# First keys in a software pipeline on VectorE, and pads of the first values cleared on ScalarE

## Reference

```python
kv = (cond @ Wkv + bkv).reshape(1, -1, 2, H, hd)     # 16 heads of 16
k, v = kv[:, :, 0], kv[:, :, 1]
k = _fq_sym(k, axis=-1)      # per row and head: s = max|k|/127, round(k/s)*s
v = _fq_sym(v, axis=2)       # per channel: the maximum runs over all 12808 rows
attn = softmax(einsum('bhqd,bhkd->bhqk', q, k)); out = einsum(attn, v)
```

## Time and profile before

| what | value |
|---|---|
| median of 3 runs | 6314.11 us (6314.06 to 6315.52) |
| the profiled execution's own time | 6316.26 us |
| its span in the trace | 6314.5 us |
| granted clock of PE, mean | 0.938 |
| busy: PE, DVE, ACT, POOL | 5663.1, 5327.8, 4621.8, 3820.7 us |

### The profile page before, as it was taken

The page is one execution under the profiler, slowest core; times in us unless marked ns, Lnnn a source line. Parts: engine busy times, 40 slices in busy tenths (PEclk is TensorE's granted clock), DMA queues, the critical chain, the costliest instruction groups (busy, mean ns, idle before and its releaser), DMA issues. The chain is left out here.

```text
span 6314.5 us, 180489 instructions
## 1 busy us (share of the span) xinstructions
PE 5663.1 (90%) x64257; PEld 2223.0 (35%) x64264; DVE 5327.8 (84%) x8826; ACT 4621.8 (73%) x4630; POOL 3820.7 (61%) x4116
## 2 busy tenths in 40 slices
PE   8787399999999999999999999999999694699974
PEld 5565123333323332332332332333233443354442
DVE  4187799999989998999999998999899535577778
ACT  4466039999989998998998998999899321366644
POOL 5433138888888887888888888888888200100000
PEclk9899569999999999999999999999999797799987
DMA  6655400100101101001011010110110101877750
GB/s 230 258 133 123 133 15 10 26 15 17 26 8 25 20 11 27 15 17 24 7 28 19 12 26 11 22 22 8 28 17 13 38 1 34 125 116 114 114 93 21
DMA packets 178691, 315.60 MB, mean 50 GB/s; under 512 B 91555, under 2 KB 137636, under 8 KB 173170
## 3 DMA queue, kind: packets, MB, share of 16 engines
q1 hardware_dynamic: 177768, 303.45, 22.9%
HBM read 198.26 MB, written 113.07 MB: 49 GB/s over the span
## 5 line engine op out<-in xcount | busy, mean ns | idle before, releaser
L1426 DVE TENSOR_REDUCE a_mx<-PS 128x1 f32<-128x512 f32 x6620 | 3984.5, 679 | 220.2 <-PE PS L1310 216.5
L1397 ACT ACTIVATE a_e<-PS,a_sk 126x1024 f32<-126x1024 f32 x3264 | 3630.6, 1113 | 386.2 <-PE PS L1293 133.0
L1164 POOL TENSOR_SCALAR a_p<-a_e 126x1024 f16<-126x1024 f32 x3264 | 3410.4, 1045 | 570.3 <-ACT a_e L1397 345.3
L1310 PE MATMUL PS<-a_K,a_Q 48*128 48x512 bf16 (+1 forms) x6884 | 2106.8, 383 | 33.1 <-POOL a_K L1129 32.4
L1293 PE MATMUL PS<-a_Q,a_K 54*128 54x512 bf16 x6528 | 1979.0, 383 | 33.5 <-issue 24.2
L1337 PE MATMUL PS<-a_e,a_sel 126*32 126x256 f32 x26112 | 1990.6, 381 | 0.0
L1333 PE MATMUL PS<-a_p,a_V 128*32 128x256 f16 x13056 | 959.0, 284 | 44.6 <-issue 32.2
L1293 PEld LDWEIGHTS PS<-a_Q,a_K 54*128 54x128 bf16 x6528 | 369.3, 94 | 1384.1 <-issue 1321.5
L1333 PEld LDWEIGHTS PS<-a_p,a_V 128*32 128x32 f16 x13056 | 337.3, 93 | 1376.2 <-issue 1291.5
L1337 PEld LDWEIGHTS PS<-a_e,a_sel 126*32 126x32 f32 x26112 | 755.4, 110 | 7.9 <-issue 1.4
L2326 DVE TENSOR_REDUCE b_mx<-PS 128x1 f32<-128x512 f32 x803 | 504.3, 683 | 188.3 <-PE PS L2210 188.1
(11 more groups left out here) (339 smaller groups left out, 3454.7 us busy)
## 6 DMA issues: line engine op xcount, KB each, us to landing
b_K<-d_k SPq DMA_DIRECT2D x210, 200.1 KB, 6.1
a_K<-d_k SPq DMA_DIRECT2D x99, 400.2 KB
b_V<-d_v SPq DMA_DIRECT2D x36, 832.0 KB, 12.2
d_k<-k_T SPq DMA_DIRECT2D x100, 252.0 KB, 4.4
d_k<-k1p SPq DMA_DIRECT2D x16, 1200.8 KB, 6.1
d_v<-v1v SPq DMA_DIRECT2D x24, 768.0 KB, 7.8
a_V<-d_v SPq DMA_DIRECT2D x68, 204.0 KB, 2.9
d_v<-vq SPq DMA_DIRECT2D x17, 803.2 KB
```

The lines of the kernel that those rows point to most:

```text
L1164: g.tensor_scalar(p[0:rows, kk % RE, :], e[0:rows, kk % RE, :], 1.0, SHIFT, ALU.mult, ALU.add).then_inc(rounded, 1)
L1310: last = pe.matmul(self.PS[:, M_BANK + j % sh.SLOTS, c0:c0 + wd], Qb[M_ROWS, ii % 4, t * P:(t + 1) * P], Kb[M_ROWS, (ii // NC) % 2, k0:k0 ...
L1397: a.activation(e[0:r, kk % RE, :], self.PS[0:r, e_bank(i, s):e_bank(i, s) + 2, :], ACT.Exp, scale=skb[0:r, hb, s:s + 1]).then_inc(exp_done, 1)
L1426: v.tensor_reduce(mx[:, col:col + 1], bank, AX.X, ALU.max).then_inc(max_done, 1)
```

## The change

1. First keys, DVE: no operation waits for the one just before it. Each raises a semaphore of its own (`k_largest`, `k_scale`, `rk_ready`, ...), and the next one of the same group stands two or more operations later in the queue, with operations of the two or three groups before in between. The separate semaphore instructions are gone. The group's last part is made three rounds after its maximum.
2. The buffers of parts (`parts`, `ip`) are four instead of two (RP = 4), and PE turns group g-4 behind kv(g), instead of g-2.
3. First keys, ACT: values(g), evacuate(g-4), high(g-1), middle(g-2).
4. PE waits only for the four clearings of `pick`, and DVE splits the bias before it waits for POOL's clearings.
5. First values: POOL no longer clears `vq`. ACT writes zeros to the 16-column pads alone, and PE's sums and SP's first store wait for that. The rounding operations raise `done` themselves. ACT issues 17 of the 34 corrections' DMAs.
6. First attention: the pad of `Kb` is cleared before `p`, and PE waits for `init` at 4, without `p`.

```diff
-            RC = 6
+            RC, RP = 6, 4
...
-                pe.wait_ge(zeroed, 10)
+                pe.wait_ge(zeroed, 4)
...
-                    if g >= 2:
-                        turn(g - 2)
-                turn(NG - 2)
-                turn(NG - 1)
+                    if g >= 4:
+                        turn(g - 4)
+                for g in range(NG - 4, NG):
+                    turn(g)
...
+                def over(g, op, signal):
+                    todo = spans(g)
+                    for s, n in todo[:-1]:
+                        self.link(v, op(s, n), self.dv)
+                    op(*todo[-1]).then_inc(signal, 1)
...
+                for g in range(NG + 3):
+                    when(g, largest_key)
+                    when(g - 1, whole)
+                    when(g, scale)
+                    when(g - 1, larger_value)
+                    when(g, reciprocal)
+                    when(g - 1, scaled)
+                    when(g, multiplied)
+                    when(g - 2, rest)
+                    when(g - 3, last)
...
+                for g in range(NG + 4):
+                    when(g, values)
+                    when(g - 4, evacuate)
+                    when(g - 1, high)
+                    when(g - 2, middle)
...
-                g.memset(vq[:, :, :, :], 0.0).then_inc(zeroed, 1)
...
+                a.activation(vq[:, :, :, HD:2 * HD].rearrange("p h t d -> p (h t) d"), along(self.onesf[:, 0:HD], 1, HEADS // 2 * NKT),
+                             ACT.Copy, scale=0.0).then_inc(pads, 1)
+                a.wait_ge(ready, 1)
+                store_corrections(a, 1)
...
-                g.memset(p[96:P, :, :], SHIFT).then_inc(init, 1)
                 g.memset(Kb[0:E_ROWS, :, sh.NK:sh.NK + PAD], 0.0).then_inc(init, 1)
+                g.wait_ge(init, 4)
+                g.memset(p[96:P, :, :], SHIFT).then_inc(init, 1)
...
-                pe.wait_ge(init, 5)
+                pe.wait_ge(init, 4)
```

More of the change, by code:

```diff
@@ L800, in scales, with reciprocal @@
+                def reciprocal(g):
+                    v.wait_ge(k_scale, g + 1)
                     if g >= 2:
                         v.wait_ge(ip_ready, g - 1)
[L802 to L808, removed]
-                        if s.stop == GT:
-                            v.sem_inc(rk_ready, 1)
-                        self.link(v, v.tensor_tensor(by_head(tmp[0:n, b, s, :]), by_head(ps), along(rc, 3, HD), ALU.mult), self.dv)
@@ L843, in scaled @@
-                def scaled(g):
-                    b = g % 2
-                    for s, n in spans(g):
-                        sc = sk[0:n, :, g * GT + s.start:g * GT + s.stop].rearrange("p h t -> p t h")
-                        self.link(v, v.tensor_tensor(by_head(kf[0:n, b, s, :]), by_head(parts[0:n, b, INT, s, :]), along(sc, 3, HD), ALU.mult), self.dv)
-                    v.sem_inc(to_cast, 1)
-                for g in range(NG):
-                    scales(g)
-                    if g >= 1:
-                        rest(g - 1)
-                    whole(g)
-                    if g >= 1:
-                        last(g - 1)
-                    scaled(g)
-                    largest(g)
@@ L859, in _, with multiplied @@
-                rest(NG - 1)
-                last(NG - 1)
+                    over(g, lambda s, n: v.reciprocal(rk[0:n, g % 2, s, :], scale_of(g, s, n)), rk_ready)
+                def multiplied(g):
+                    v.wait_ge(rk_ready, g + 1)
+                    if g >= 2:
+                        v.wait_ge(k_whole, g - 1)
+                    over(g, lambda s, n: v.tensor_tensor(by_head(tmp[0:n, g % 2, s, :]), by_head(keys_of(g, s, n)),
+                                                         along(rk[0:n, g % 2, s, :], 3, HD), ALU.mult), kv_seen)
@@ L862, in _ @@
+                v.wait_ge(v_larger, NG)
             @block.scalar
@@ L896, in _, with when @@
                 a.wait_ge(zeroed, 10)
[L897 to L909 removed]
+                def when(g, op):
+                    if 0 <= g < NG:
+                        op(g)
+                for g in range(NG + 4):
[3 more added lines that the diff above has]
+                    when(g - 2, middle)
     def first_values(self):
@@ L1026, in _ @@
                 sp.wait_ge(ready, 1)
[L1027 to L1031 removed]
+                store_corrections(sp, 0)
                 sp.wait_ge(stored, 16 * (17 + 2 * (HEADS + 1)))
```

130 lines of the change are left out of this document (67 added, 63 removed).

## The result

| kernel | median (lowest to highest), runs | against before, 95% interval |
|---|---|---|
| before | 6314.82 us (6314.06 to 6318.07), 4 | |
| changed | 6220.11 us (6216.75 to 6225.9), 4 | 0.985 (0.9833 to 0.9867) |

What follows compares the result with a forecast made beforehand. It took DVE's chain to hold a first-keys group at 6.27 us, with PE the next bound. Keys -61.2, start +1.4, values -26.6 and attention -5.2 sum to -91.6 us: 6222.5 from 6314.1, range 6208 to 6248 (0.8).

Steps and rivals of the forecast that it cites:

- Keys, -61.2: First keys: the stage from PE's first product to ACT's last copy falls from 334.2 to 273.0 us.
- P = 4.97: First keys: time of one steady group, 4.97 us instead of 6.27, counted for 46 groups.
- POOL's lock: First keys: POOL and DVE exclude each other for whole operations, costing DVE from nothing to five times 0.1 us.
- The groups without turns and the tail: First keys: first group 7.1 us, four groups without turns 15.6, and a tail of four turns with copies 21.7.
- Start, +1.4: Start of the first keys: DVE's cast is held by POOL's clearing of `k_parts`, so PE begins 1.4 us later.
- Values, -26.6: First values: no clearing of `vq` and corrections issued by two queues; the end comes at 703.7 instead of 730.3 us.
- one shared pace: First values: alternative in which both issuers of the corrections share one pace, so the gain is -19.8 us.
- Attention, -5.2: Start of the first attention: PE is released by loads of `a_K` at about 739 instead of 744.26 us.
- (a): First keys: DVE becomes the bound at 5.5 us a group, stage 298 us, kernel 6247.5; chance 0.17 with its halfway case.
- (b): First keys: POOL starves between DVE's operations, a group takes 8.8 us and the kernel 6413; chance 0.03.
- (c): First keys: stores or loads bound, a group takes 5.6 us and the kernel is near 6252; chance 0.07.
- (d): Whole kernel: the changed stages do not hold what they promise and the time stays near 6314 us; chance 0.02.

Runs made afterwards that it cites:

- linked version: The changed kernel with every DVE operation of the first keys also waiting for its own end before the next may start; 6249.23 us.
- version with additions: The changed kernel with ACT clearing `k_parts`, second-half roundings waiting only for their own head's store, and turns of groups 48 and 50 in free banks; 6216.14 us.
- single parts: Three kernels, each the kernel before with only the changed first keys, first values or order of POOL's clearings in the first attention; 6251.1, 6291.49 and 6303.91 us.

## Why the prediction was right

**What bounds.** Right: DVE's chain before, PE after. I had traced PE's wait of 1.16 us back over ACT to a late DVE, and then still spoke of it as something that ACT's order takes away. The order alone takes nothing away (ratio 1.0); it is what the pipelined version needs (49 us).

**Keys, -61.2, measured -62.0.** The term P = 4.97 came out at 4.95 by two errors that cancel. I put PE's own time at 4.89, since I read four tiles as four times 0.977; from the end of the turns to the next ones it is 3.96 (422.64 to 426.60), so PE needs 4.95. And I gave POOL's lock 0.08 us of a group, between my bounds, where it costs the group nothing: DVE's round is 4.37 us, below the 4.47 that I had without POOL, and what the lock costs DVE (`last` takes 0.73 us where it took 0.69 in the linked version) goes out of DVE's idle time. Even with DVE busy all the time it is some 0.14 us, far from my upper bound of 0.5. The groups without turns and the tail together were right to 0.1 us, 22.3 and 22.1 against 22.7 and 21.7, the tail with some luck: I had only its last turn at the half clock and steps of 3.4 us, and three turns ran at it, two steps of 4.45.

**Start, +1.4, measured +1.5.** The held cast, taken from line 949, showed as expected: 3.25 us, and a second one of 1.60.

**Values, -26.6, measured -24.3.** The second half's start moved by 19.1 us against 18.8, and the last issue came 74.6 us into the block, where I had it at 74.5. Two independent issuers were right, and not one shared pace. What failed is the last step of this term: I let the block end right behind the last issue, as before, and with two queues it ends 2.3 us later than that, because the semaphore of the landings comes late. This is the whole miss. (ACT's zeros, 13 us by my estimate, took 11.1; the 8 us of room that I gave them were 9 by my own numbers.)

**Attention, -5.2, measured -6.0.** The loads decided, as I had it, and released PE 3.9 us behind the first issue. I took the middle between two ends, and the early end (-6.3) was nearer.

**Rivals.** (a) needs links, not DVE as such: with the links put back the stage takes 300.4 us, where I had 298, and the kernel 6249, where I had 6247.5. Without them DVE has 0.58 us to spare. The Trainium skill, "VectorE: DVE Perf Modes", section "The DRAIN you can't avoid", by which nothing is saved by dropping the semaphores, doesn't hold for this chain: 5.44 us a group with them and 4.37 for the round without. The same section adds that a next operation that is not held starts earlier, and points to "Two Vector instructions with no wait between them" for when it is held; with that the trace agrees (0.60 us between starts for a record of 0.69). (b) is refuted. (c) didn't come about: the DMA share is 0.72, as forecast at 0.7, and no copy waits for a store except in the tail of the version with additions. (d) is refuted by the single parts.

**The total.** -90.8 us at the attention's first product against a forecast of -91.6. That it came so near is luck in part: values 2.3 us too good, keys and attention 0.8 us each too poor, start 0.1 too good. What lies behind is scatter: the runs gave -94.7 in the first set and -86.3 in the last.

## What to carry over

When a wait names an engine, ask whether that engine's own loop is closed before you cost the wait: here the engine that waited and the one it waited for both had slack, and the third one set the pace. In a chain of short operations on one engine, look first for separate semaphore instructions (0.11 us each here) and then for links to the operation just before (0.12 us each). And when you add a second queue for many small DMAs, read the issues in short windows, since an average hides a slow start, and cost the time until the semaphore has counted the last landing as well as the issuing.

## What I had not expected of the hardware

- GpSimd's small operations find room between VectorE's even when VectorE has no idle time at all (50.00 of 50 us busy), and cost it little (0.63 to 0.67 us from start to start where they end, 0.60 elsewhere); GpSimd's chain grows from 2.64 to between 3.1 and 3.3 us.
- Two queues that issue DMAs of 6.5 KB side by side hardly slow each other (ten in 4.6 and 4.3 us, one queue alone 4.5), but with two the semaphore of the landings gets its last update 3.25 us behind the last issue, with one 0.97, while the packets end 0.6 us behind it in both.
- The granted clock fell for a moment in the middle of a stretch in which PE was busy 19.4 of 20 us, in some executions and not in others of the same kernel, at a cost of 1.6 us each time.
